# Loading, normalising and transposing x and ctx inside attention 0, by DMA transposes, instead of ahead of it by TensorE

## What is computed

```
x = x + attention0(layernorm(x), ctx)     # 32 query heads and 8 key/value heads of 128, softmax over 64 keys
x = x + ffn0(layernorm(x))                # 8-bit quantised weights and activations, inner size 1792
x = x + attention1(layernorm(x), ctx)     # heads of 16
x = x + ffn1(layernorm(x))                # 512 x 512, gated by 64 clusters
```

## Time and profile before

| | before |
|---|---|
| median of 3 runs | 1799.95 us (1799.30 to 1800.84) |
| the profiled execution | 1798.56 us, of which the span from the first to the last instruction is 1796.5 us |
| PE busy, share of the span | 1618.1 us, 90% |
| DVE busy | 1298.1 us, 72% |
| ACT busy | 781.5 us, 44% |
| POOL busy | 307.5 us, 17% |
| mean granted TensorE clock | 0.965 of full speed |

### The profile page before, as it was taken

The page is one execution under the profiler, slowest core; times in us unless marked ns, Lnnn a source line. Parts: engine busy times, 40 slices in busy tenths (PEclk is TensorE's granted clock), DMA queues, the critical chain, the costliest instruction groups (busy, mean ns, idle before and its releaser), DMA issues. The chain is left out here.

```text
span 1796.5 us, 30331 instructions
## 1 busy us (share of the span) xinstructions
PE 1618.1 (90%) x11222; PEld 888.4 (49%) x11238; DVE 1298.1 (72%) x2434; ACT 781.5 (44%) x1678; POOL 307.5 (17%) x259
## 2 busy tenths in 40 slices
PE   4899999999999999999999669999997796889786
PEld 3455555555555555555555235555554353555443
DVE  6567667776776676767668488988877535999687
ACT  3424243434242433333433256667665223565442
POOL 2001000010000000100000111111110224777510
PEclk9899999999999999999999889999999898999988
DMA  6122321212222213131202200000002001000002
GB/s 246 24 71 48 84 55 53 71 48 72 71 58 73 59 48 95 24 105 39 69 22 97 94 2 1 1 1 0 0 0 59 0 1 36 0 0 0 0 1 94
DMA packets 147871, 81.81 MB, mean 46 GB/s; under 512 B 113202, under 2 KB 129587, under 8 KB 147508
## 3 DMA queue, kind: packets, MB, share of 16 engines
q1 hardware_dynamic: 108868, 47.20, 9.7%
q10 hardware_dynamic: 38896, 33.03, 5.8%
HBM read 44.57 MB, written 11.53 MB: 31 GB/s over the span
## 5 line engine op out<-in xcount | busy, mean ns | idle before, releaser
L528 PE MATMUL pj<-XT,WQ 128*128 128x512 f16 x1536 | 338.1, 380 | 6.4 <-PEq L330 6.4
L570 PE MATMUL xp<-WO,OT 128*128 128x512 f16 x1536 | 338.3, 380 | 1.8 <-DVE X L801 1.8
L570 PEld LDWEIGHTS xp<-WO,OT 128*128 128x128 f16 x1536 | 147.8, 98 | 183.5 <-issue 11.4
L528 PEld LDWEIGHTS pj<-XT,WQ 128*128 128x128 f16 x1536 | 148.4, 98 | 181.5 <-DVE WKV L294 6.7
L645 ACT ACTIVATE E<-E 128x512 f32<-128x512 f32 x64 | 40.2, 628 | 345.1 <-DVE E L739 345.1
L801 DVE SCALAR_TENSOR_TENSOR X<-xp,X 128x512 f32<-128x512 f32 x128 | 88.2, 690 | 119.0 <-PE xp L570 117.9
L508 POOL TENSOR_TENSOR VW<-VW,XB 128x1024 f32<-128x1024 f32 x14 | 33.0, 2356 | 768.9 <-DVE VW L107 768.9
L910 PE MATMUL db<-W0T,XD 128*128 128x448 f16 x768 | 159.7, 359 | 0.0
L936 PE MATMUL eb<-W1T,DT 128*128 128x512 f16 x672 | 150.7, 383 | 3.7 <-DVE DT L1086 2.6
L704 DVE SCALAR_TENSOR_TENSOR QT<-pj,QT 128x512 f16<-128x512 f32 x128 | 88.1, 688 | 67.0 <-ACT QT L628 66.6
L910 PEld LDWEIGHTS db<-W0T,XD 128*128 128x128 f16 x768 | 76.5, 100 | 70.9 <-issue 5.3
(11 more groups left out here) (227 smaller groups left out, 2663.5 us busy)
## 6 DMA issues: line engine op xcount, KB each, us to landing
W0T<-in_L_xattn_wq ACTq DMA_DIRECT2D x7, 1024.0 KB, 5.3
W0T<-in_L_xattn_wo ACTq DMA_DIRECT2D x7, 1024.0 KB, 5.0
CS<-in_ctx SPq DMA_DIRECT2D x4, 1024.0 KB, 10.1
X<-in_x SPq DMA_DIRECT2D x4, 1024.0 KB, 11.2
out<-X SPq DMA_DIRECT2D x8, 512.0 KB, 3.6
XB<-in_L_ffn_W ACTq DMA_DIRECT2D x28, 128.0 KB, 2.7
w0t<-XB ACTq DMA_DIRECT2D x7, 512.0 KB, 3.3
w1t<-W0T ACTq DMA_DIRECT2D x7, 512.0 KB, 3.8
```

Of the source, the lines that this page charges most:

```text
L528: last = pe.matmul(bank[:, :], w, src[:, b, k, tokens], start=n == 0, stop=n == 3 * KC - 1)
L570: last = pe.matmul(xp[i % 2][:, :], OT[:, a, j, i * P:(i + 1) * P], WO[:, b, j, :], start=n == 0, stop=n == 3 * REP - 1)
```

## The change

The stage ahead is gone. Its work is now inside attention 0:

- **Block 0 first.** SP issues x block 0, wq, ctx block 0 (4 DMAs of one tile) and wk, wv. The other loads (x and ctx blocks 1 to 3, wo) are issued by ACT, between its first instructions.
- **Split, then transpose.** The 32 units now run in the order of `RUNS`: x0, c0, x1, c1, x2, c2, c3, x3. The high and low parts are made first, from the float32 tile in SBUF, into one of 4 slots of a new buffer XH: the high part on ACT (`split_high`), the low part on DVE for the first 12 units and on POOL for the other 20. SP then transposes each part from XH straight into XT or CT with a DMA transpose of 128 x 512 float16: 64 of them. A slot is used again once both its transposes have landed (`turned`).
- **Where it stands.** x0, c0, x1 and c1 go ahead of the first block step, between the projections of block 0; x2, c2 and c3 are split in block step 0, x3 in block step 1. The layernorm statistics of block 3 go into block step 1.
- **Waits.** PE waits for all 8 transposes of x's block before projection unit 0 of that block, and for those of ctx's block before unit 4 (group 0 only). Unit 0 waits for the split of wq alone, unit 4 for that of wk and wv.
- **Group 0** is written out, and the loop runs over groups 1 to 6.
- The context tiles wait for their turn in memory that attention 0 uses later (OT, WO, parts of XB and VW).

```diff
+        RUNS = (("x", 0), ("c", 0), ("x", 1), ("c", 1), ("x", 2), ("c", 2), ("c", 3), ("x", 3))
+        ON_VECTOR = 3 * BT
...
         @block.sync
         def _(sp):
+            load_x(sp, 0)
+            load_q(sp, 0)
+            load_context(sp, 0)
+            load_kv(sp, 0)
+            def turn(kind, blk):
+                for n in run_units(kind, blk):
+                    i = UNITS[n][1]
+                    for part in range(2):
+                        if part == 0:
+                            sp.wait_ge(S["split_hi"], n + 1)
+                        else:
+                            wait_split_lo(sp, n)
+                        sp.dma_start_transpose((XT if kind == "x" else CT)[:, part, :, i * P:(i + 1) * P],
+                                               XH[:, n % 4, part, :]).then_inc(turned[n % 4], 16)
...
+            def split_high(kind, blk):
+                for n in run_units(kind, blk):
+                    if kind == "x":
+                        act.wait_ge(S["xn_done"], UNITS[n][1] + 1)
+                    else:
+                        act.wait_ge(c_ld[blk], LOADED[blk] if blk else 16 * BT)
+                    if n >= 4:
+                        act.wait_ge(turned[n % 4], 32 * (n // 4))
+                    act.activation(XH[:, n % 4, 0, :], unit_source(n), ACT.Copy).then_inc(S["split_hi"], 1)
...
-            high(0, 0, range(6))
-            with act.Fori(0, GROUPS - 1) as g:
+            act.wait_ge(x_ld[0], 16)
+            load_x(act, 1)
+            stats_scalar(act, 0, (0,))
+            high_q(act, 0)
+            load_context(act, 1)
+            load_o(act, 0)
+            split_high("x", 0)
+            load_x(act, 2)
+            split_high("c", 0)
+            load_context(act, 2)
+            high_kv(act, 0)
+            load_context(act, 3)
+            load_x(act, 3)
+            high(0, 0, (0,))
+            stats_scalar(act, 0, (1,))
+            high(0, 0, (1, 2))
+            split_high("x", 1)
+            high(0, 0, (3,))
+            split_high("c", 1)
+            stats_scalar(act, 0, (2,))
+            high(0, 0, (4, 5))
+            group(0, False)
+            with act.Fori(1, GROUPS - 1) as g:
```

On POOL a normalised tile of x is written when both splits of the tile two before it are done, since there are two XN buffers; from x2 on POOL alternates between normalising a tile and making a low part:

```diff
+            def normalised(i):
+                pool.wait_ge(stats_ready, i // BT + 1)
+                if i >= 2:
+                    before = unit_of("x", i - 2)
+                    pool.wait_ge(S["split_hi"], before + 1)
+                    wait_split_lo(pool, before)
...
+            dve.wait_ge(x_ld[0], 16)
+            moments(dve, 0, 0)
+            scales(dve, 0, 0)
+            low_q(dve, 0)
+            split_low("x", 0)
+            split_low("c", 0)
+            low_kv(dve, 0)
+            dve.wait_ge(x_ld[1], LOADED[1])
+            moments(dve, 0, 1)
+            low(0, 0, 0)
+            scales(dve, 0, 1)
+            low(0, 0, 1)
+            low(0, 0, 2)
+            split_low("x", 1)
+            low(0, 0, 3)
+            dve.wait_ge(x_ld[2], LOADED[2])
+            moments(dve, 0, 2)
+            low(0, 0, 4)
+            scales(dve, 0, 2)
+            low(0, 0, 5)
```

205 lines of the change are left out of this document (115 added, 90 removed).

## The result

The changed kernel took 1804.7 us (median of 20 runs, 1801.82 to 1812.41), the kernel before 1799.54 us (20 runs, 1797.68 to 1801.76). The ratio is 1.0033, with a 95% interval of 1.0024 to 1.0042: slower by 5 to 6 us, where I had forecast 1779, that is 20.7 us faster, and a range that ended at 1791. The profiled execution has a span of 1802.0 us and a mean granted clock of 0.961.

A forecast was written before the change was run, and what follows sets the result against it. Attention 0 was taken to go at PE's pace. First scores earlier (-28.2 us), block step 0 (+4.1, +1.5, +0.6) and block step 1 (+1.3) summed to -20.7: 1799.95 became 1779.2, rounded to 1779, range 1771 to 1791.

The forecast's parts named there:

- a small transpose was priced by its bytes: SP's issue of a 128x512 transpose: taken as 0.8 us, between bounds of 0.65 and 1.31 us.
- transposes beside loads were given half of the DMA engines: Stage ahead: x0's transposes share with ACT's loads, so 4.7 us for eight become 9.4 from 14 on.
- x first, at 24 us: Start of the kernel: PE's first projection begins at 24 us, where it began at 56.2 before.
- 4.0 us of waits up to the first scores: First projection to first scores: 17.0 us as before plus 4.0 of waits, putting the scores at 45.0.
- Block step 0, +6.2: Block step 0: PE stall behind ACT's x2 splits +4.1 us, lower clock after it +1.5, later softmax weights +0.6.
- Block step 1, +1.3: Block step 1: ACT's root waits for DVE's moments of block 3, delaying k; +1.3 us (0 to 2).
- SP's order is harmless here: Block step 0: SP's 32 transposes end about 3 us after the scores, softmax weights come at 9.4 us; no cost.
- Block step 2, 0: From block step 2 on: the streams are the same as before, so no change in time, 0 us.
- Behind the last scores of attention 0, 0: Everything behind attention 0: the same as before, 0 us.
- Number 2: SP's queue: a small transpose costs as much as a large one, 1.31 us; total 1788 us, chance 0.20.
- Number 3: Stage ahead: transposes stand behind loads issued before them, x0's last landing at 28; +4 us, 1783, chance 0.11.
- Number 4: SP's transposes do not overlap, one every 2.9 us; 1860 us, gain used up from about 1.65 us; chance 0.04.

The follow-up runs named there:

- e1_merge: Changed kernel with both parts of a unit in one 128x1024 transpose, 32 in all: 1798.15 us, 0.9994 of the kernel before.
- e2_quarter: Changed kernel with each part in two 128x256 transposes, 128 in all: 1866.69 us, 1.0367 of the kernel before.
- e3_quiet: Changed kernel with wo, ctx block 3 and x block 3 loaded just ahead of block step 0, second group's wo in block step 2: 1796.03 us.
- e4_lowq: Changed kernel with the low part of wq on DVE behind x0's low parts instead of ahead: 1807.67 us, 1.0042 of the kernel before.
- e6_late: Changed kernel with ACT's splits of x2 and x3 behind the first output's high part, not ahead of k's: 1799.68 us, 0.9997 of the kernel before.
- e5_merge_quiet: Changed kernel with the edits of e1_merge and e3_quiet together: 1790.25 us, 0.9943 of the kernel before.
- e12_wo1: Changed kernel with only the second group's wo load moved, from block step 1 to block step 2: 1802.15 us, 1.0014 of the kernel before.
- e7_three: Changed kernel with the edits of e1_merge, e3_quiet and e6_late together: 1788.44 us, 0.9935 of the kernel before.
- e9_c3: e7_three with the last two tiles of ctx block 3 split and transposed in block step 1 instead of 0: 1785.43 us, 0.9913 of the kernel before.
- e10_first: e9_c3 with k's high part of block 0 ahead of ACT's c1 splits, and x2's moments and root in block step 0: 1788.43 us.
- e11_first_warm: e10_first with 172 transposes of the identity on PE ahead of the first projection: 1807.08 us, 1.0035 of the kernel before.
- e8_three_warm: e7_three with 96 transposes of the identity on PE ahead of the first projection: 1788.93 us, 0.9937 of the kernel before.

## Why the prediction was wrong

Two steps of the prediction failed, and terms 1, 2 and 5 below rest on them: a small transpose was priced by its bytes (0.8 us of SP, found 1.27 in the median), and transposes beside loads were given half of the DMA engines (found: a fifth of their time, and none of it in some stretches). The miss of 26 us is the sum of these terms: 23.7 us by the scores of block step 4 (a lead of 20.7 was forecast, a lag of 3.0 was found; block step 3 gave 0.5 back) and 2.6 behind.

1. **x first, at 24 us: found 28.45 (+4.5).** The failed step is the size of a small transpose: I took 0.8 us because "the work goes with the bytes", but SP's issue does not go with the bytes. It is 1.27 us at 128x512, and was the same for half and for twice the size (e1_merge, e2_quarter). Beside loads it was 1.7 us (13.66 for eight), for which I had kept only the DMA engines' own share. And that share was the second failed step: I had written "if SP's transposes get half of the engines", from 14 on. They began behind wk and wv, the first landing at 22.1, and then had 0.20 of the engines' time against the loads' 0.90 (19 to 20 us). With fewer loads (e3_quiet) x came at 25.76, so that some 2.7 of the 4.5 us are the loads', by one execution of each; moving wk and wv was not tried. The last low part of x0 ended at 19.2 where I had 17.7; e4_lowq, in which it ended at 16.5 and nothing came sooner, showed that this did not matter.
2. **4.0 us of waits up to the first scores: found 11.5 (+7.5).** The sum has 4.23 us for c0 at unit 4, which my working did not hold at all, since c0's transposes at 0.8 us were hidden; it was for their landing, beside ACT's loads of ctx block 3 and x block 3. Then 3.63 us for k, of the kind I had named. With 0.35 us at unit 2 that makes 8.2. The rest, some 3 us, is PE's own time: the first four units took 7.84 + 5.35 = 13.2 us against 11.90 in the earlier trace rows (the first twelve matmuls began 0.43 us apart, in the kernel before the first seven, and the others 0.22 apart), and unit 4 took 4.36 behind its wait, where the same twelve matmuls take 2.75 us at full clock (the e1_merge row above).
3. **Block step 0, +6.2: found +9.6 (+3.4).** Place and mechanism were right: 5.21 us ahead of the second weighing, released by DVE's low part, behind ACT's splits (forecast 4.1, bounds 1.2 and 7). ACT's chain of four splits took 6.9 us rather than 5.4, from 71.05 to 77.92; 1.3 us of the 1.5 is one subtract of POOL that took 2.43 us instead of 1.16, beside DVE's low part of wo (70.88 to 73.16). What I undersized more was the clock: 12.56 us for `project_out` behind the stall, where it takes 10.53 at full clock (granted 0.50 from 82 to 84, 0.83 in the mean until 96.5), and 11.35 for the projections behind the scores, where they take 10.52 (0.87 from 56.9 to 70.5). e6_late confirms it: with the splits elsewhere, 33.1 us.
4. **Block step 1, +1.3: found +2.3 (+1.0).** The wait was another one: SP still had c3 to issue when the softmax weights were ready (85.75 + 23.01 = 108.76, PT at 108.80), 2.20 us on PE. I had written "SP's order is harmless here". That was said of block step 0, where it held, and I never drew SP's queue for block step 1. The sixteen took 23.0 us, where sixteen at 1.3 are 20.8; the load of the next group's wq, issued at 98.04, moved beside the last seven.
5. **Block step 2, 0: found +7.8.** The largest single miss. That "the streams are the same as before" was true of the instructions but not of the DMA engines: x3's transposes were issued from 119.17 to 130.57, and wo's load, which had been there before as well, was moving beside them; four of the eight landed only behind it, from 131.86 to 134.57. 5.45 us of waiting, and 2.2 more at the lower clock (12.75 us instead of 10.52; granted 0.82 in the mean). e5_merge_quiet removed nearly all of it, e1_merge none, e12_wo1 about 3 us.
6. **Behind the last scores of attention 0, 0: found +2.6**, with no new wait. Behind waits of the same length as before, the same instructions took longer: the last `project_out` 12.60 us against 11.43 (granted clock 0.83 and 0.92), and the first twelve large matmuls of ffn0 4.12 against 3.59 (0.59 and 0.67); over these the lag grows from 2.9 to 4.4 us. So 1.5 us of it is the clock coming back later, and the rest stays open. Between the versions this part takes 803.5 to 806.5 us, with no order that follows from their edits, so it is not shown that the change brings it.

**The rivals.** Number 2, SP's pace, had the right mechanism and was given 0.20: it put SP at 1.31 us, the scores at 49 and x3 late by 2 us. What it lacked is that the same instruction beside loads is slower again, and that each new wait costs a piece of clock on top. Number 3, transposes behind the loads, happened in part. Between 19 and 20 us SP's queue and ACT's moved 173 and 171 packets, and between 24 and 25 us 165 and 169. By the rule of the Trainium skill (DMA: Bandwidth & Descriptors, section on queues, rings and completion order) each DMA engine takes turns, packet by packet, between the rings of SP and ACT, and those stretches agree with it. But I had read equal turns as equal halves, and with packets of 256 bytes against 2048 they are not. From 126 to 128 us the trace does not agree with turns: the transposes issued from 124.35 on did stand behind wo's load. Number 4, the slow side, needed 1.65 us per transpose. It was 1.65 to 1.7 for the first three runs of units and 1.3 to 1.5 later, and I had given this case 0.04. What it forecast, 1860, did not come, because the slow pace did not last. The row that should have moved that chance was already on the table: 1.31 us in the earlier trace rows is four fifths of the way to that threshold, with few loads beside it (a DMA share of 0.39).

**The range** failed because I took a value near half (0.8 us) as the likely one between two bounds of which only one was a measured instruction. With 1.31 us in the sum, rival 2 becomes the forecast, 1788, and the result is still 17 us above it. e3_quiet, which keeps the 64 transposes and takes loads away from beside them, came out at 1796: so the loads that it moved are some 9 of those 17 us, and the rest is in waits that neither sum had. That e5_merge_quiet and e7_three stand at 1788 to 1790 is a coincidence: they have half as many transposes as rival 2.

The idea of the change is sound: e9_c3 does the same work inside attention 0, in half as many transposes and another order, and is 0.87% faster than the kernel before, 15.7 us of the 20.7.

## What to carry to other kernels

A DMA transpose between SBUF buffers was priced on SP by the instruction, not by the byte: merge parts until the waits, not the number of issues, set the end. Beside loads of large packets, do not give it half of the DMA engines: here it moved at 42 to 44 GB/s instead of 244, and the load that PE needs last is the one to keep out of its way. When work moves from a quiet stage into a full one, draw every in-order queue it enters (SP's issues, ACT's order, and the DMA engines with the loads already in them) for every block step it touches, not only for the first. An order edit that takes away one wait is worth what the next wait leaves: e6_late's edit on top of e5_merge_quiet, and e10_first's on top of e9_c3, each removed about 5 us at one place, and the total kept nothing measurable of it while the next cause stayed.

## What was unexpected in the hardware

- **A short DVE operation lasts as long as POOL's subtract beside it.** Operations on 128x16 elements that take 0.17 us alone took 0.96 to 1.13 us, each ending within 0.07 us of a subtract of POOL of 1.15 us; with the subtracts cut to 0.2 us they took 0.17 again. The Trainium skill (SBUF — State Buffer, who interferes with whom) states an exclusive lock on the port pair that the two share, held for a whole instruction, which DVE takes for an operation with two SBUF inputs or in one of its two-port modes. The meeting ends agree with such a lock, and not with a share of bandwidth; in which mode the slowed operations with one input (L72, L82, L84) ran, no trace here shows.
- **172 more instructions ahead of a loop cost some 20 us inside it.** e11_first_warm differs from e10_first by these alone, and PE stood still eight times for up to 2.2 us in the scores at the start of later groups, with nothing it waited for: 13.1 us, and with the slower matmuls behind each stop (11.96 to 12.21 us for projections of 10.52) its last scores of attention 0 come 20.8 us later. That it is the loading of PE's instructions is my guess. The trace has DMAs of 16 KB on a queue of the kind "instruction" next to these stops (one until 297.5 and one from 299.6 on, for the stops that end at 299.0 and 302.1), but e10_first has them too, at 298.7 and 302.4, and did not stop; e8_three_warm, with 96 more, had none of the stops. Where the loop lies against whatever unit is loaded was not tried.
- **The same stage ahead took 28.5 to 31.3 us** in profiled executions of the same instructions (the changed kernel and e12_wo1), by the pace of x0's transposes alone. A forecast of a stretch in which loads and transposes meet should not claim to know it better than by 3 us.
